# Attention followed by a mixture of experts on one core: TensorE's bounded program without its loop, and one division and store of attention moved into the next head pair

## The reference, cut to what matters

```python
# x: (4, 1024, 256), ctx_1024: (4, 77, 256), 16 heads of 64, all in float32
x = x + xattn(ctx_1024, layernorm(x), mask)       # attention
x = x + moe(layernorm(x))                         # one shared and eight routed experts, two per token

# in xattn, b, h, d = 4, 16, 64; scale = d ** -0.5
q = (ln @ Wq); k, v = split(concat([xn @ Wkv, ln @ Wkv]))      # 1024 queries, 77 + 1024 keys
qn = rmsnorm(q, qn_g) * scale;  kn = rmsnorm(k, kn_g)
attn = softmax(where(mask, qn @ kn.T, -max))
out = attn @ v                                     # then out @ Wout + bout
```

## Time and profile before

| what | us |
|---|---|
| median of three runs | 2600.8 |
| the profiled execution | 2599.2 |
| its span in the trace | 2597.4 |
| TensorE busy | 2426.4 (93%) |
| VectorE busy | 1811.9 (70%) |
| ScalarE busy | 1705.9 (66%) |
| GpSimd busy | 1190.5 (46%) |
| mean granted TensorE clock | 0.982 of full |

### The profile page before, as it was taken

The page is one execution under the profiler, slowest core; times in us unless marked ns, Lnnn a source line. Parts: engine busy times, 40 slices in busy tenths (PEclk is TensorE's granted clock), DMA queues, the critical chain, the costliest instruction groups (busy, mean ns, idle before and its releaser), DMA issues. The chain is left out here.

```text
span 2597.4 us, 55511 instructions
## 1 busy us (share of the span) xinstructions
PE 2426.4 (93%) x20310; PEld 2014.8 (78%) x20310; DVE 1811.9 (70%) x2452; ACT 1705.9 (66%) x2286; POOL 1190.5 (46%) x783
## 2 busy tenths in 40 slices
PE   4799999999999999999999999997989999999998
PEld 3677677777776777777777777665989999999997
DVE  7667767677667766776667766775876566767775
ACT  2677777888887887777778777783333334444453
POOL 4334433444334433443344433442533526666665
PEclk8899999999999999999999999998999999999999
DMA  6322332233223332233223322246732459999996
GB/s 196 138 81 81 117 107 79 87 115 107 87 79 113 100 96 86 83 118 104 79 87 115 107 87 79 86 119 129 165 92 72 139 176 321 322 319 318 325 321 173
DMA packets 231564, 363.77 MB, mean 140 GB/s; under 512 B 59559, under 2 KB 139739, under 8 KB 227400
## 3 DMA queue, kind: packets, MB, share of 16 engines
q1 hardware_dynamic: 204694, 301.66, 37.7%
q0 software_dynamic: 25696, 58.82, 8.0%
q10 hardware_dynamic: 978, 0.34, 0.1%
HBM read 280.90 MB, written 79.85 MB: 139 GB/s over the span
## 5 line engine op out<-in xcount | busy, mean ns | idle before, releaser
L718 DVE TENSOR_TENSOR pr_lo<-ps_s,pr_hi 128x1024 fp32r<-128x1024 f32 x416 | 505.0, 1220 | 287.0 <-ACT ps_s L829 287.0
L828 ACT ACTIVATE pr_hi<-ps_s 128x1024 fp32r<-128x1024 f32 x512 | 526.2, 1028 | 231.9 <-PE ps_s L972 160.8
L1008 PE MATMUL ps_o<-pr_hi,vA 64*65 64x512 f32 x2292 | 489.7, 399 | 52.5 <-DVE pr_lo L718 31.6
L1008 PE MATMUL ps_o<-pr_lo,vA 64*65 64x512 f32 x2292 | 483.0, 392 | 0.0
L1008 PE MATMUL ps_o<-pr_hi,vC 64*65 64x512 f32 x2292 | 482.1, 391 | 0.0
L460 POOL TENSOR_TENSOR rs<-ss,minus_half 128x16 f32<-128x16 f32 (+1 forms) x96 | 225.7, 2351 | 480.8 <-DVE ss L693 480.8
L1666 ACT ACTIVATE ht<-f_ps_h,b 128x256 f32<-128x256 f32 x440 | 184.6, 471 | 341.6 <-PE f_ps_h L1598 341.6
L829 ACT ACTIVATE ps_s<-ps_s 128x1024 f32<-128x1024 f32 x384 | 392.5, 1022 | 0.0
L458 POOL TENSOR_TENSOR sq<-raw 128x1024 f32<-128x1024 f32 (+1 forms) x96 | 166.2, 1731 | 436.9 <-ACT raw L773 436.9
L1598 PE MATMUL f_ps_h<-xT_hi,w 128*128 128x256 f32 x1760 | 355.4, 285 | 3.6 <-DVE xT_lo L1700 3.1
L718 DVE TENSOR_TENSOR pr_lo<-pr,pr_hi 128x1024 fp32r<-128x1024 f32 x160 | 241.0, 1508 | 159.1 <-ACT pr L829 154.5
(11 more groups left out here) (220 smaller groups left out, 4611.8 us busy)
## 6 DMA issues: line engine op xcount, KB each, us to landing
w<-w1S_dram SPq DMA_DIRECT2D x160, 512.0 KB, 6.0
lnT_sb<-lnT_dram SPq DMA_DIRECT2D x31, 2304.0 KB, 9.6
w2raw<-in_L_ffn_Wproj SPq DMA_DIRECT2D x78, 512.0 KB, 6.8
w1S_dram<-cut POOLq DMA_DIRECT2D x36, 512.0 KB, 3.0
rec<-rden_dram SPq DMA_DIRECT2D x63, 256.0 KB, 3.8
routed_dram<-empty POOLq DMA_DIRECT2D x28, 387.0 KB, 3.6
xt<-routed_dram SPq DMA_DIRECT2D x39, 258.0 KB, 6.6
w_raw<-in_L_xattn_Wkv SPq DMA_DIRECT2D x66, 128.0 KB, 4.0
```

The source lines that it names most:

```text
L718: v.tensor_tensor(pr_lo[:, ring(w, d), :], full_of(d), pr_hi[:, ring(w, d), :].bitcast(F32), ALU.subtract).then_inc(s_lo, 1)
L828: act.activation(pr_hi[:, ring(w, d), :], ps_s[:, d % 2, :], ACT.Exp, bias=bias)
L1008: ins = mm(ps_o[0:DH + 1, h, :], v_[rows, h], p_[rows, 512 * h:512 * h + 512], start=k == 0 and part == 0 and i == 0, stop=k == KT - 1 and ...
```

## The change

TensorE's bounded program calls `window` for v = -1 to 15 in Python, so that no hardware loop is left in it; its general program and all other engines keep their loops. The division of the first half goes from after `pr_lo` of unit 16 to after `pr_lo` of unit 7 of the next window, and its store from behind `broadcast(w, 0, 0)` to between `spread` and `broadcast` of the second half in the next window. The very last window keeps the old place for its own first half.

```diff
@@ sync, window(w)
                 if w.attend and not w.first:
                     spread(w, 1, 1)
+                    store(w, 0, 1)
                     broadcast(w, 1, 1)
@@
                         store(w, 1, 1)
                     spread(w, 0, 0)
                     broadcast(w, 0, 0)
-                    store(w, 0, 0)
+                    if closing(w) and w.s == 1:
+                        store(w, 0, 0)
@@ vector, window(w)
                             if d == 5:
                                 invert(w, 1, 1)
-                            if d == 9:
-                                divide(w, 1, 1)
+                            if d in (7, 9):
+                                divide(w, (d - 7) // 2, 1)
                         if w.attend and d == 13:
                             invert(w, 0, 0)
-                        if w.attend and d == 16:
+                        if closing(w) and w.s == 1 and d == 16:
                             divide(w, 0, 0)
@@ tensor, pe_windows(general)
-                windows(pe, window)
+                if general:
+                    windows(pe, window)
+                else:
+                    for v in range(-1, WINDOWS // 2):
+                        for s in range(2):
+                            window(Window(v, s))
```

## The result

The changed kernel takes 2620.3 us (median of four runs, 2617.41 to 2625.5) where the kernel before takes 2602.2 in the same comparison: the ratio is 1.0073, 95% interval 1.0055 to 1.009. It is slower by 0.7%; forecast was no change, 2598.2, with a range of 2578 to 2616. The profiled execution took 2625.5 us and is the slowest of the four, so the two traces lie 26.3 us apart where the medians lie 18.1.

A forecast was written before the change was run, and what follows sets the result against it. TensorE was taken as the bound, standing still in attention only at window edges. Gains of 7.9 and 34.2 less losses of 32.8 and 6.7 gave 2.6 us gained: 2598.2 us, "the same", range 2578 to 2616.

The forecast's parts named there:

- The loop: TensorE's 13 jumps back in attention end with their waits for instructions: 7.9 us gained, 1.2 us left for VectorE's loop.
- the straight program doesn't starve: Rival denied here: TensorE's fetch can't keep up beside load_ln, a 2 us gap each window, 2660; chance 0.04.
- The edge: At 30 window edges `pr_lo` of unit 17 ends 1.14 us earlier with the division gone: 34.2 us gained.
- nothing at the edge: Rival: GpSimd's squares keep VectorE anyway, `pr_lo` of unit 17 ends as before: 2632; counted with the slower ones.
- The chain through `rec`: From `pr_lo` of unit 7 to the second division 9.6 us, 1.13 us too late in 29 windows: 32.8 us lost.
- VectorE's idle time before the second division: Sign in the profile: VectorE idle about 1.0 to 1.1 us there, released by the landing of `rec`.
- a put that isn't held: Case within the short-wait rival (chance 0.34): with `rec` landing in 3.4 us, only 0.1 us lost a window, 2569.
- the squares in 14 windows: Case within the slower rival: the second division stands behind GpSimd's squares, 4.4 us lost in each of 14 windows, 2646.
- The slower rival: VectorE waits long for `rec` at unit 9: 2607.5 at 4.1 us; from 5.2 us it meets GpSimd's squares; chance 0.26.
- fetching is no new traffic: Written-out code needs no more instruction packets: 7 in 105 us against 9 in the loop.
- The last two windows: Windows 30 and 31, without projection and with shorter units, wait 3.2 and 3.5 us for the second division: 6.7 us lost.
- Both at nothing: In SyncE's queue load_ln is issued some 9 us earlier and load_w 9 us later, neither costing anything.

The follow-up runs named there:

- a: The kernel before with only TensorE's program written out, division and store as before: 2586.99 us, ratio 0.9953.
- c: The changed kernel with the first half's division at unit 6 instead of unit 7, store and put following it: 2559.09 us, ratio 0.9843.
- d: The changed kernel with the first half's store issued behind the second half's broadcast: 2561.57 us, ratio 0.9851.
- g: The kernel before, TensorE's loop kept, with load_ln issued ahead of the first half's store: 2646.7 us, ratio 1.017.
- h: The kernel before with load_ln ahead of the first half's store and TensorE's program written out: 2586.52 us, ratio 0.994.
- i: The changed kernel with GpSimd's first load for the experts held until the 61st reciprocal of attention: 2612.82 us, ratio 1.0055.
- b: The changed kernel with TensorE's loop put back, only division and store moved: 2709.48 us, ratio 1.043.
- e: The changed kernel with a second buffer for `rec` and the first half's store moved down behind load_w: 2557.7 us, ratio 0.9826.

## Why the prediction was wrong, point by point

**The loop: too small.** Forecast 7.9, measured 10.8 inside attention and 13.7 on the medians (a). The 1.2 us that I let stay for VectorE's loop were taken off twice: its jumps cost 4.6 us in all (a), but they are in the windows of before as in those of a, and so already in a clean window's 52.5 (a's mean is 52.47). With 52.47 and without the 1.2 the 27 windows give 10.0. ("With the 2.29 us each" was a slip besides: the earlier trace rows give 2.1 us in the mean of ten. It entered no sum.) In TensorE's waits no "issue" gap and no dip at the edges is left, as forecast; the straight program doesn't starve.

**The edge: right.** Forecast a stall of 0.52 us in place of 1.66 and 1.14 us at each of 30 edges; measured 0.53, and 1.13 a window between a and c. The waits say it too: 53.3 - 19.4 = 33.9 us, with c's line:

```profile
PE ps_o L1012 <- DVE pr_lo L720: 19.4, 31, 3.4
```

That `pr_lo` takes the division's place behind GpSimd's squares was the right reading, and the rival "nothing at the edge" is out. The division at unit 7 takes its 1.21 us beside quiet engines, as said.

**The chain through `rec`: right in every link, too short in two of them.** This is the step that failed most, "Sum 2.36 + 0.26 + 3.2 + 3.8 = 9.6", and with it the 32.8 us that follow from it: the wait cost 57.1. From the start of `pr_lo` of unit 7 to the second division, the median over windows 1 to 29 is 10.09 us:

| link | forecast | median of 29 windows |
|---|---|---|
| to the issue of the store | 2.62 | 2.59 |
| store to `rec`'s issue, put held | 3.2 | 3.51 |
| `rec` to the second division | 3.8 | 3.94 |

The put waits behind the store, as I had it: 2.61 to 2.67 us in 27 of 31 windows, and 1.56 with the store behind it (d). But 3.1 us of landing and 0.1 was too little: the store lands after 3.19, and `rec` is issued 0.3 behind that; whether the 0.3 is the put's own time no run shows. The half microsecond on a chain that was 1.1 us too long already makes it 1.6, and that is what an ordinary window loses: the median of windows 1 to 29 is 53.04 us against c's mean of 51.34, so 1.7.

VectorE's idle time before the second division was forecast at 1.0 to 1.1 us; by my own terms it was 919.04 less the end of the work before, about 2.1, a slip in the working that changed no sum. Measured are 1.94 to 2.91 in the windows 2 to 29 whose put is not a long one. TensorE's stall before the half's first values was forecast at 0.8 and is 0.92 in the window shown, 1.22 in the median of 29; the 0.3 before `scores` of unit 12 isn't there, since in that window it follows the 0.92 without a gap. Two of the rivals' sums are a little off too: a put that isn't held gives 2566 to 2568 by the terms of the working, not 2569 (d, where the put isn't held, measured 2561.57), and the squares in 14 windows give 2644, not 2646.

**The cliff: named, but from the wrong link.** The slower rival said that a second division late enough meets GpSimd's squares and stands there. In two windows of after it does, for 2.37 and 2.59 us where it takes 1.22, and a third window is long as well. The worst, VectorE and GpSimd, then TensorE:

```profile
665.51 2.58 DVE L685 TENSOR_TENSOR o_second<-o_second,rec 64x1024 f32<-64x1024 f32 x1 [3.96 <-DMA rec<-rden_dram]
```
```profile
665.13 1.88 POOL L460 TENSOR_TENSOR sq<-raw 128x1024 f32<-128x1024 f32 x1 [14.67 <-ACT raw L775]
```
```profile
669.37 0.69 PE L1010 MATMUL ps_o<-pr_hi,vA 64*65 64x512 f32 x2 [3.91 <-DVE o_first L651]
```

Behind the 3.91 us TensorE's clock is at its lower level for a while:

```profile
665.00:675.00 10.00, 6.09 (x31) 4.04 (x31) 6.78 (x5) 2.43 (x3) 1.88 (x1) 0.67 0.21 47
```

In these two windows the put took 4.07 and 4.17 us (issued at 386.65 and 657.53). In the third it took 2.66; the division took its 1.22 us and GpSimd's squares were the ones that stood (2.25 us instead of 1.89), but the clock dipped there too, behind this stall:

```profile
611.93 0.44 PE L1010 MATMUL ps_o<-pr_hi,vA 64*65 64x512 f32 x2 [1.42 <-DVE o_first L651]
```

Forecast were no dips of the clock inside attention; from 200 to 1700 us of after it falls in these three windows and nowhere else. These windows take 57.12, 55.01 and 57.75 us, 15.9 more than three of c's, so some 5.3 each where I had written 4.4, which counted the squares and not the clock. I had asked whether the landing of `rec` would reach 5.2 us, and it never did (4.29 at most); it was the put that was late.

Why a put takes 3 to 4 us now and then the trace at least hints at. While each late put of these windows was under way, a 16 KB packet of the instruction queue started, 1.91 and 1.97 us behind the put's issue. The queues from 386.6 to 390.8 us of after:

```profile
q8 instruction: 1, 0.02, 1.4%
```

From 200 to 1690 us, four puts of `den` in after took over 3 us, and each has such a packet between its issue and that of `rec`; of the other 52 one has. In c it is eight of the ten long ones. The packets are not more numerous than before (135 in the whole of after, 164 in the kernel before), as the prediction said; but "fetching is no new traffic" left out where they fall. In the two kernels with TensorE's loop and the old divisions, before and g, no put of `den` in that stretch takes over 1.7 us; in a and h, where only TensorE's program is written out besides, some take 3.10 to 3.70. They hit nobody there. This is a coincidence in the traces, strong but not tried by a run of its own.

**The last two windows: a term missed.** Forecast 6.7 lost, measured (52.52 + 46.39) - (43.46 + 43.61) = 11.9. I had counted `rec` against GpSimd's load, not the put and the store, which the move had placed in the same moment as the load of the shared expert's weights. That explains 2.7 us of window 30, by i; but with the load held the two windows are still more than 11 longer than in a. What the rest of their cost is made of, no run separates.

**The sum again.** Between the first and the last copy of `o_second` lie 29 windows with projection and the last two. After has 1644.96 - 52.52 - 46.39 = 1546.0 us in the 29, c 1581.83 - 49.88 - 43.09 = 1488.9, a 1608.57 - 43.46 - 43.61 = 1521.5. So what was measured is 10.8 for the loop, 1521.5 - 1488.9 = 32.6 for the edge, -57.1 for the wait and -11.9 for the last two: -25.6, all of it. Forecast were 7.9, 34.2, -32.8 and -6.7. The wait alone is 24.3 us larger, 2.0 a window instead of 1.13: some 29 x 0.49 = 14 by the longer chain, and the rest by the three long windows.

**The coupling that I had costed at nothing.** "is issued some 9 us earlier" and "Both at nothing" were right only because the other half of the change took the jumps away. With the jumps it costs some 44 us (g), and the move without the program written out is b, 109 us slower. So writing out TensorE's program is worth 13.7 us by itself and 89 beside the move (2709.5 - 2620.3): two parts of one change were not to be priced one by one. Of b's loss, some 44 us are this, as far as g's jumps are like b's; the rest must hold the wait for `rec`, 90.9 us of VectorE's idle time, and the four windows of b in which the second division stands behind the squares (a stall of TensorE of 3.81 us at 351.88 among them), but no run separates these.

## What to carry to other kernels

When a step is moved ahead of a shared buffer's next use, write the chain out to the consumer and compare its length with the slack, then ask for the tail: a chain within a microsecond of its limit pays at each window for each tenth that it is too long, and beyond the limit there may be a second price (here GpSimd's squares, then the clock). Ask for the tail of every link: here it was the small put, not the large transfer. Before taking a wait as given, look at what stands in it for no reason: one store ahead of a 4 KB put on the same queue made this change 0.7% slower instead of 1.5% faster, and a second buffer of 256 KB 1.7% faster (e). And a DMA that moves to another place in its queue is also moved in relation to every other engine's jumps.

## What the runs showed of the hardware that was not expected

- At a jump back TensorE stood 1.7 to 2.3 us with the 2.3 MB load issued behind it, and 4.1 to 5.2 us with that load under way (g, b); in g and b there was a stretch at the lower clock at every jump. Written out, the same code beside the same load shows no gap (h). A jump of VectorE shows a gap of 0.35 us (a).
- A 4 KB put issued 0.9 us behind a 256 KB store of the same queue is through in 2.6 us instead of 1.56, and never in less. The Trainium skill (DMA: Bandwidth & Descriptors, Queues, rings and completion order) has each DMA engine take turns, packet by packet, between the queues it has work for. By that a load on another queue delays a put too, and the trace agrees: 7.15 us beside GpSimd's load of 512 KB, 4.62 with that load held back (i).
- A 4 KB put that overlapped a 16 KB packet of instructions took 3.6 to 4.2 us in after (four of the five that did).
- A wait of TensorE of about 4 us was followed by a mean granted clock of 0.67 over the next ten microseconds, so its price was more than its length. One wait of 1.42 us was followed by 0.83 over ten microseconds (612 to 622), while of a's 30 waits of 1.66 us at the edges none was. The length of the wait alone doesn't tell which.
